# Turning queries, keys and probabilities by row halves in a float32 attention and feed-forward kernel

## The reference

```python
x = x + cross_attention(layernorm(x), ctx)     # 8 heads of 64, 77 context rows per sequence
x = x + two_layers(layernorm(x))               # the stage that matters here
# one layer, windows of 128 rows, so a sequence has two:
h = shift_token(x); q, k, v = split(h @ wqkv)  # 256 -> 3 * 512
q, k = rotary_xpos(l2norm(q) * qs, l2norm(k) * ks)
sim = q @ k.T * 8, masked to the own and the previous window
x = x + softmax(sim) @ v @ wo
h = layernorm(shift_token(x)) * g + b
a, g = split(h @ w1 + b1)                      # 256 -> 2 * 682
x = x + (a * gelu(g)) @ w2 + b2
```

## Time and profile before

| | before |
|---|---|
| time, median of 3 runs | 1366.84 us (1365.93 to 1367.32) |
| the profiled execution | 1370.5 us, of which the span (first to last instruction) is 1368.5 us |
| the 32 iterations of the layers | from about 266 us on to the end |
| busy in the span | PE 98%, PEld 90%, DVE 76%, ACT 69%, POOL 58% |
| mean granted clock of PE | 0.999 of full speed |

### The profile page before, as it was taken

How to read it: one execution, slowest core, us unless ns; L and a number is a source line. 1 busy time by engine, 2 the same in 40 slices (tenths; PEclk the granted TensorE clock), 3 DMA queues, 4 the chain that set the end, 5 groups by cost and what they waited for, 6 DMA issues and landing times.

```text
span 1368.5 us, 32692 instructions
## 1 busy us (share of the span) xinstructions
PE 1340.9 (98%) x11503; PEld 1232.9 (90%) x11503; DVE 1033.6 (76%) x3003; ACT 939.0 (69%) x2662; POOL 798.3 (58%) x640
## 2 busy tenths in 40 slices
PE   8999999999999999999999999999999999999997
PEld 7999898779999999999999998899999999999987
DVE  5777765678777777777777878877777777777774
ACT  6887776577666666666666777766666666666672
POOL 1221221566666666666666767866666666666653
PEclk9999999999999999999999999999999999999999
DMA  5323112100111111100001211111111111111101
GB/s 178 104 93 109 61 48 102 56 20 31 31 31 31 31 30 29 29 29 29 29 30 31 73 31 39 39 39 39 38 38 38 37 37 37 37 37 38 31 31 33
DMA packets 50517, 63.41 MB, mean 46 GB/s; under 512 B 8403, under 2 KB 32105, under 8 KB 50409
## 3 DMA queue, kind: packets, MB, share of 16 engines
q1 hardware_dynamic: 50408, 61.99, 14.6%
HBM read 38.17 MB, written 16.78 MB: 40 GB/s over the span
## 4 chain that ended last, share of the span: by engine, by line
PE 77%; ACT 8%; DVE 7%; POOL 4%; issue 2%; DMA 2%; SPq 0%; POOLq 0%; DVEq 0%
PE pb L571 37%; PE pb L909 8%; PE pb L840 6%; PE pb L923 6%; PE pb L857 6%; PE pb L872 4%; PE pb L947 4%; ACT x_p L1112 4%; PE pb L884 2%; ACT x_pt L1118 2%; POOL n_inv L1843 1%; DMA x_in<-x 1%; PE pb L796 1%; PE pb L585 1%; POOL r_cos L1855 1%
## 5 line engine op out<-in xcount | busy, mean ns | idle before, releaser
L1251 ACT ACTIVATE p_t<-p_t,s_nm 128x128 f32<-128x128 f32 (+1 forms) x512 | 226.1, 446 | 11.8 <-DVE s_nm L1619 9.4
L571 PE MATMUL pb<-h_hi,w_hi 128*128 128x256 f32 x704 | 209.3, 297 | 1.5 <-DVE h_lo L1583 1.2
L1843 POOL TENSOR_TENSOR n_inv<-n_cl,half_neg 128x16 f32<-128x16 f32 x64 | 205.7, 3213 | 5.3
L571 PE MATMUL pb<-h_hi,w_lo 128*128 128x256 f32 x704 | 198.4, 282 | 0.0
L571 PE MATMUL pb<-h_lo,w_hi 128*128 128x256 f32 x704 | 198.4, 282 | 0.0
L1879 POOL TENSOR_TENSOR hg_lo<-hg,hg_hi 128x256 fp32r<-128x256 f32 (+1 forms) x192 | 143.2, 754 | 67.6 <-DVE hg_hi L1650 67.6
L1848 POOL TENSOR_TENSOR r_cos<-r_cos,r_sin 128x1024 f32<-128x1024 f32 x64 | 158.0, 2469 | 14.3 <-DVE r_sin L1606 13.5
L571 PE MATMUL pb<-wqkv_hi,xt_hi 128*128 128x512 f32 x384 | 162.8, 424 | 0.2 <-DVE xt_lo L1374 0.2
L1619 DVE CUSTOM_DVE_ANT_0 p_t<-pb,mask_t 128x128 f32<-128x128 f32 (+1 forms) x512 | 149.2, 352 | 17.1 <-PE pb L840 16.9
L1643 DVE SCALAR_TENSOR_TENSOR hg<-pb,b_t,gl 128x256 f32<-128x256 f32 (+1 forms) x192 | 91.7, 478 | 87.8 <-ACT gl L1234 65.4
L571 PE MATMUL pb<-wqkv_lo,xt_hi 128*128 128x512 f32 x384 | 152.1, 396 | 0.0
(11 more groups left out here) (147 smaller groups left out, 3961.9 us busy)
## 6 DMA issues: line engine op xcount, KB each, us to landing
y_state<-x SPq DMA_DIRECT2D x32, 256.0 KB, 2.0
x_cur<-y_state SPq DMA_DIRECT2D x32, 256.0 KB, 2.6
x_res<-y_state SPq DMA_DIRECT2D x32, 256.0 KB, 2.8
x_in<-x SPq DMA_DIRECT2D x16, 256.0 KB, 2.9
x_state<-x SPq DMA_DIRECT2D x16, 256.0 KB, 2.0
x_orig<-x_state SPq DMA_DIRECT2D x16, 256.0 KB, 2.9
out<-x SPq DMA_DIRECT2D x16, 256.0 KB, 2.2
x<-x SPq DMA_DIRECT2D x32, 112.0 KB, 2.3
```

The lines of the kernel that those rows point to most:

```text
L571: mm = pe.matmul(dst, s, m, start=(n == 0 and k == 0), stop=(n == len(pairs) - 1 and k == 2))
L1251: e = nc.scalar.activation(pu, pu, ACT.Exp, bias=s_nm[:, j, k:k + 1], scale=-1.0, accum_out=s_sum[:, j, k:k + 1])
L1843: nc.gpsimd.tensor_tensor(n_inv[:, t], n_cl[:, t], half_neg[:], ALU.pow).then_inc(pool_inv, 1)
```

## The change

Turns are made by row halves: `half_turn` turns rows 0 to 63 of the data into one bank and rows 64 to 127 into the same columns of a second bank, by two transposes of 64 rows with 64 moving columns. The probabilities are turned in three pairs of units (`turn_p_two`), each pair over the same two banks, and ACT copies both units of a pair when both are turned, reading the two banks in runs of 64 columns. Pair 0 stands where turn_p(1) stood, pair 2 where turn_p(2) and (3) stood, pair 4 where turn_p(5) stood. Queries and keys are turned in two halves of eight turns each. Each score product is made as two products of 64 query columns. A table `PHYS` renumbers the banks (4 to 7, 5 to 4, 7 to 5) in every use. Waits are merged accordingly, and a semaphore increment stands between them and the first instruction of each such burst. Where the query and key banks of one row tile are not neighbours, `rotate` makes two instructions of one (item 0 alone).

```diff
+        PHYS = [0, 1, 2, 3, 7, 4, 6, 5]
-        PT_BANK = [5, 7, 5, 7, 4, 7]
-        QT_BANK = [5, 3, 7, 2]
+        PT_BANKS = slice(4, 6)
+        QT_BANKS = [slice(3, 5), slice(5, 7)]
...
+            def half_turn(banks, col, source):
+                for row in range(2):
+                    rows = slice(row * DH, row * DH + DH)
+                    mm = pe.transpose(pb[:, (banks.start, banks.stop - 1)[row], col:col + DH], source(rows),
+                                      ones_at[rows, rows])
+                return mm
...
# scores
+                pe.sem_inc(scores_go, 1)
...
-                        mm = pe.matmul(pb[:, S_BANK[u], k * keys:k * keys + keys], qk_t[r:r + DH, 0, ch, q_cols],
-                                       qk_t[r:r + DH, 1, ch, 0:keys], start=True, stop=True)
+                        for rows in (slice(0, DH), slice(DH, P)):
+                            mm = pe.matmul(pb[rows, PHYS[S_BANK[u]], k * keys:k * keys + keys],
+                                           qk_t[r:r + DH, 0, ch, q_cols.start + rows.start:q_cols.start + rows.stop],
+                                           qk_t[r:r + DH, 1, ch, 0:keys], start=True, stop=True)
...
+            def turn_p_two(a, b, d, u):
+                pe.wait_ge(dve_pn, at(b, UNITS, u + 2))
+                if u == 0:
                     pe.wait_ge(dve_max, at(b, UNITS, 5))
+                    if d is not None:
+                        pe.wait_ge(dve_x2, at(d, 1, 1))
+                elif u == 2:
+                    pe.wait_ge(act_pt, at(b, UNITS, 2))
+                else:
+                    pe.wait_ge(act_pt, at(b, UNITS, 4))
+                pe.sem_inc(halves_go, 1)
+                for i in range(2):
+                    for k in range(4):
+                        mm = half_turn(PT_BANKS, (4 * i + k) * DH,
+                                          lambda rows: p_t[rows, u + i, k * P:k * P + P])
+                    mm.then_inc(pe_pt, 1)
...
+            def turn_qk(a, b, c, half):
+                if half == 0:
                     pe.wait_ge(pool_qk, at(a, NT, NT))
                     if b is not None:
+                        pe.wait_ge(act_pt, at(b, UNITS, UNITS))
+                    if has_next(a):
+                        pe.wait_ge(act_xhi, at(plus(a, 1), 1, 1))
+                        pe.wait_ge(dve_xlo, at(plus(a, 1), 1, 1))
+                else:
+                    if b is not None:
+                        pe.wait_ge(dve_olo, at(b, 2, 2))
+                        pe.wait_ge(dve_x1, at(b, 1, 1))
+                pe.sem_inc(halves_go, 1)
+                for j in range(4):
                     for t in range(NT):
+                        mm = half_turn(QT_BANKS[half], (j * NT + t) * DH,
+                                          lambda rows: r_cos[rows, t, (4 * half + j) * P:(4 * half + j) * P + P])
                 mm.then_inc(pe_qkt, 1)
...
# PE's order in run_l
                 if b is not None:
-                    turn_p(a, b, d, 0)
...
-                    turn_p(a, b, d, 1)
+                    turn_p_two(a, b, d, 0)
...
-                    turn_p(a, b, d, 2)
-                    turn_p(a, b, d, 3)
-                    turn_p(a, b, d, 4)
+                    turn_p_two(a, b, d, 2)
                 if c is not None:
                     hidden(a, b, c, 2)
                 if b is not None:
-                    turn_p(a, b, d, 5)
+                    turn_p_two(a, b, d, 4)
...
# ACT
+            def probs_copy_two(b, u):
+                act.wait_ge(pe_pt, at(b, UNITS, u + 2))
+                for i in range(2):
+                    nc.scalar.activation(p_t[:, u + i].rearrange("p (m h n) -> p h m n", h=2, n=DH),
+                                         pb[:, PT_BANKS, i * T:i * T + T].rearrange("p h (m n) -> p h m n", n=DH),
+                                         ACT.Copy).then_inc(act_pt, 1)
```

More of the change, by code:

```diff
@@ L577, in idle_products @@
                 for _ in range(n):
-                    pe.transpose(pb[:, b, 0:P], id_f, id_f)
+                    pe.transpose(pb[:, PHYS[b], 0:P], id_f, id_f)
+            def half_turn(banks, col, source):
[4 more added lines that the diff above has]
+                return mm
             def turn_x(n):
@@ L622, in x_probs @@
                 for k in range(4):
-                    mm = pe.transpose(pb[0:CTX, u % 2, k * P:k * P + P], x_p[:, u, k, :], id_f)
+                    mm = pe.transpose(pb[0:CTX, PHYS[u % 2], k * P:k * P + P], x_p[:, u, k, :], id_f)
                 mm.then_inc(x_ptr, 1)
@@ L1015, in run_l @@
                     feed(b, c, d, 4)
-                if b is not None:
-                    turn_p(a, b, d, 0)
                 if a is not None and not is_first(a):
@@ L1596, in rotate @@
                 half = DH // 2
-                first = qkv_bank(a, t, 0)
-                qk = pb[:, first:first + 2].rearrange("p j (h d) -> p j h d", d=DH)
+                first, second = PHYS[qkv_bank(a, t, 0)], PHYS[qkv_bank(a, t, 1)]
+                qk = [pb[:, first].rearrange("p (h d) -> p h d", d=DH), pb[:, PHYS[second]].rearrange("p (h d) -> p h d", d=DH)]
                 for j in range(2):
                     nc.vector.tensor_tensor(r_cos[:, t, j * INNER:j * INNER + INNER].rearrange("p (h d) -> p h d", d=DH),
-                                            qk[:, j], cos_t[:, ly, t, j].unsqueeze(1).broadcast_to([P, HEADS, DH]), ALU.mult)
+                                            qk[j], cos_t[:, ly, t, j].unsqueeze(1).broadcast_to([P, HEADS, DH]), ALU.mult)
                 for s in range(2):
                     o = r_sin[:, t].rearrange("p (j h d) -> p j h d", j=2, d=DH)[:, :, :, s * half:s * half + half]
-                    i = qk[:, :, :, half - s * half:DH - s * half]
                     w = sin_t[:, ly, t, :, s * half:s * half + half].unsqueeze(2).broadcast_to([P, 2, HEADS, half])
-                    e = nc.vector.tensor_tensor(o, i, w, ALU.mult)
+                    if second == first + 1:
+                        i = pb[:, first:first + 2].rearrange("p j (h d) -> p j h d", d=DH)
+                        e = nc.vector.tensor_tensor(o, i[:, :, :, half - s * half:DH - s * half], w, ALU.mult)
+                    else:
+                        for j in range(2):
+                            e = nc.vector.tensor_tensor(o[:, j], qk[j][:, :, half - s * half:DH - s * half], w[:, j], ALU.mult)
                 e.then_inc(dve_rope, 1)
@@ L1642, in gate @@
                     dve.wait_ge(pool_hglo, at(plus(c, -1), FC, FC))
-                nc.vector.scalar_tensor_tensor(out=hg[0:rows, m], in0=pb[0:rows, W1_BANK[m], 0:T],
+                nc.vector.scalar_tensor_tensor(out=hg[0:rows, m], in0=pb[0:rows, PHYS[W1_BANK[m]], 0:T],
                                                scalar=b1_t[0:rows, ly, 0, m:m + 1], in1=gl[0:rows, m % 3],
```

136 lines of the change are left out of this document (52 added, 84 removed).

## The result

The changed kernel took 1369.96 us (median of 17 executions), the kernel before 1366.77 in the same measurement: a ratio of 1.0024, with a 95% interval of 1.0017 to 1.0030. The profiled execution of the changed kernel took 1369.76 us for a span of 1367.7.

What follows compares the result with a forecast made beforehand. It took PE's own instruction stream to bound the kernel. Per iteration, 0.36 us saved on turns after shape changes, less a 0.39 stall, plus 0.06 on scores, gave 0.03, or 0.8 us over 32: 1366.0 us, range 1352 to 1390.

Steps and rivals of the forecast that it cites:

- A pair of half turns: Turns of probabilities, queries and keys: a pair takes 0.062 us instead of 0.109, saving 1.88 us an iteration.
- Leaving a burst: Tile-shape change after a burst of half turns: next load 0.148 us after the last pair's second turn; 0.195 us each.
- The stall of weigh_early: PE waits for ScalarE's copies of units 4 and 5 after the last half turn: 0.39 us in each iteration.
- The scores: Score products of 64 query columns, four tiles in turn: 0.06 us saved an iteration.
- The dear rivals: Half turns keep the long load or don't overlap: 1430 us, chance 0.14; scores two at a time: 1450 us, chance 0.05.
- second stall: Cover lost at the third pair of units or scores, or PE emptied inside the scores: 1373 to 1379 us, chance 0.05.
- 32 of them: In the sum: 0.03 us saved an iteration, multiplied by 32 iterations, gives 0.8 us.
- At nothing: Later data and copies for pairs, residual, semaphore increments, bank renumbering and the first item's split rotation: priced at no cost.
- the third pair's data: Unit 3's normalised probabilities: pair due at 1097.21, VectorE ends at 1097.26 with units due 2 us later; no cost.
- the copies of units 2 and 3: Two copies done at 1099.1, PE there at 1099.4: 0.3 us of cover, no cost.
- the 0.34 us at the scores: Cover for the two copies the scores await after the last half turn of queries and keys; no cost.
- the clock 1.00: Two neighbouring local-attention iterations: 34.12 us each, all of it PE, at the full granted clock.

Runs made afterwards that it cites:

- after: First of two traces of the changed kernel, with no further edit; the changed kernel took 1369.96 us, ratio 1.0024 to the kernel before.

## Why the prediction was wrong

**The terms were right.** A pair of half turns takes 0.062 us: a burst has 0.49 us between its first and last start, that is seven steps and the first load's 0.049. By the load time that the Trainium skill ("TensorE: Matmul & The Clock Gate", "LDWEIGHTS (loading the stationary operand)") gives for 128 columns, a pair would be estimated at 107 ns or more. The trace disagrees: half turns keep the short load, 0.049 us exposed and 0.062 a pair. Leaving a burst costs 0.151 us ahead of the next load, for 0.148. The stall of weigh_early is 0.43 us on the load and some 0.38 on the stream, whose first load is exposed in its place, for 0.39. The scores give 0.05, for 0.06. Together 0.05 us an iteration, for 0.03. (0.03 times 32 is 1.0 us, and the prediction wrote 0.8; nothing hangs on it.) The dear rivals are out: the pair is not 0.112 and the scores are not 5 us. No second stall came in the steady iterations.

**The step that failed is the sum's "32 of them".** It multiplied the steady iteration by all iterations of the layers, and so priced the fill and the drain like the rest. The ground was laid in the first paragraph ("a change is worth what it takes out of that stream, times about 32 iterations"), which is true only where PE's stream sets the end. In iterations 1, 2, 31 and at the end it does not: other engines do, and there shortening PE's pieces is worth little while each new wait costs its whole length. Three covers that the prediction took as given under "At nothing" were read in steady iterations: the third pair's data, the copies of units 2 and 3, the 0.34 us at the scores. Where the pipeline is not full they are gone. The run with whole turns in pairs shows it without any half: +0.9 us in iteration 1, +1.1 in iteration 2. At the scores the wait for copies of queries and keys in iteration 15 is 0.8 us where it was 0.5.

**And the clock was taken as constant.** Its "the clock 1.00" was read in two steady iterations. In the first iteration the granted clock fell to 0.50 behind the gaps of the paired half turns; filling the gaps with idle turns kept it at 1.00 and brought 2.0 us back. No term of the prediction had it, and none of its rivals. It is the larger of the two errors: with the fall of iteration 1 gone, the layers take 0.5 us more than before instead of 3.1, so the waits alone turn the forecast gain of 0.8 us into a loss of at most 0.5, and the rest of the loss came with the clock and the late transfer.

By size, mean of the two traces of each kernel: iteration 1 +1.6, iteration 2 +0.7, iteration 31 +0.3, the end +1.3, the 23 steady ones -0.8; iterations 15 to 19, which carry the change of layer, -0.1. The sum is +3.1 against a measured 3.2. Of iteration 1's 1.6, 0.15 is waiting, as the run with idle turns shows, and 1.5 the clock (2.0 in one trace, 1.0 in the other). Of the end's 1.3, 0.8 is the late transfer of one trace, half of its 1.7.

What stays open: why the fall lasts one weighing burst in one execution and three in another, and where the executions at 0.995 and 0.996, seven of the 17, lose what the two traces (0.997 and 0.998) do not show. Whether pairing with whole turns would bring the fall in iteration 1 in other executions is open too.

## What to carry to other kernels

Price a change once for the steady iteration and once for each iteration that fills or drains, because a wait that is covered in the one costs its full length in the other. Before you put a late iteration down to a cause, check it in a second trace: here a single DMA that took 3.36 us instead of 1.71 looked like an effect of the clock. Where a change opens gaps between short bursts of PE, look at the granted clock of the stretches that already have gaps; idle products in a gap, where nothing waits behind them, can keep it. And look at what a saving forces: here units had to go in pairs to share two banks, which cost more than the halves brought, and moving the pair so that its copies are covered was worth more than the whole change.

## What the runs showed of the hardware

- Two 64-row turns side by side take 0.062 us a pair where a 128-row turn takes 0.109; four 64x64 score tiles start 6 to 7 ns apart and take no longer together than two of 128 columns did.
- In iteration 1 of the changed kernel the granted clock fell from 1.00 to 0.50 at the end of a stretch of 4.00 us with PE busy for 1.38, behind a gap of 2.00 us, and stayed low, while PE was busy again, for 6.85 us in one trace and 3.5 in the other. With paired whole turns it stayed at 1.00 through the 6.00 us in which PE was busy for 3.10.
- The same fall costs little or much by where it stands: 3.5 us at 0.50 cost iteration 1 about 1.0 us (27.12 against 26.16) and 6.85 us about 2.0, while 3.45 us near the end of the run with idle turns go with an end only 0.2 us longer than that of "after", which has no fall at that place.
- One transfer of the shift took 3.36 us on the last chain of one trace of the changed kernel and 1.71 at the same place in the other.
